# An edge-attention pass whose running sums stay in two PSUM banks, with small operations moved from VectorE to TensorE, ScalarE and GpSimd

## What is computed

```python
q = (xn @ Wq + bq).reshape(n, H, DH); k = ...; v = ...      # H = 8 heads of DH = 32
ep = ef @ We + be
scores = einsum('ehd,ehd->eh', q[dst], k[src] + ep[:, None, :]) * scale * ew[:, None]
m = segment_max(scores, dst)
ex = exp(scores - m[dst])
s = segment_sum(ex, dst)
out = segment_sum((ex / s[dst])[:, :, None] * v[src], dst)
```

## Time and profile before

| What | us |
|---|---|
| median of three runs | 3732.68 |
| lowest and highest | 3732.53, 3735.69 |
| the profiled execution's own time | 3734.78 |
| its span in the profile | 3733.0 |
| PE, DVE, ACT and POOL busy, whole span | 3127.7, 2161.4, 1687.2, 1888.5 |

### The profile page before, as it was taken

How to read it: one execution, slowest core, us unless ns; L and a number is a source line. 1 busy time by engine, 2 the same in 40 slices (tenths; PEclk the granted TensorE clock), 3 DMA queues, 4 the chain that set the end, 5 groups by cost and what they waited for, 6 DMA issues and landing times. The chain is left out here.

```text
span 3733.0 us, 52272 instructions
## 1 busy us (share of the span) xinstructions
PE 3127.7 (84%) x13504; PEld 2408.8 (65%) x13504; DVE 2161.4 (58%) x4835; ACT 1687.2 (45%) x3903; POOL 1888.5 (51%) x1845
## 2 busy tenths in 40 slices
PE   2778888788878689769859999999999999659798
PEld 2567666566665578646437777777777777436565
DVE  6333334333334600075569999999999999653515
ACT  1444333333334122233246676667676676332323
POOL 2777777777772044401046666666666666120010
PEclk8778767777778599979769999999999999779899
DMA  5555555555550167641067777777777777300000
GB/s 143 148 147 146 139 153 140 154 144 142 147 141 20 44 192 218 182 167 63 9 190 218 222 219 218 214 224 218 218 216 221 221 219 209 111 24 1 22 5 35
DMA packets 345535, 547.29 MB, mean 147 GB/s; under 512 B 170928, under 2 KB 222389, under 8 KB 344967
## 3 DMA queue, kind: packets, MB, share of 16 engines
q0 software_dynamic: 113216, 348.74, 32.8%
q1 hardware_dynamic: 224312, 183.42, 16.8%
q10 hardware_dynamic: 7743, 12.07, 1.0%
HBM read 493.32 MB, written 51.90 MB: 146 GB/s over the span
## 5 line engine op out<-in xcount | busy, mean ns | idle before, releaser
L2816 POOL DMA_INDIRECT store<-kv_d,src_of x832 | 872.4, 1049 | 414.6 <-issue 242.1
L821 POOL DMA_INDIRECT agg_rows<-xn_d,src_of x832 | 800.0, 962 | 268.7 <-issue 242.3
L993 PE MATMUL agg_sums<-agg_rows,agg_member 128*128 128x257 f32 x1664 | 578.0, 501 | 181.7 <-DVE acc L885 92.4
L834 ACT ACTIVATE agg_rows<-agg_rows,weight_of 128x256 f32<-128x256 f32 x832 | 373.0, 500 | 632.1 <-DMA agg_rows<-xn_d,src_of 631.5
L993 PEld LDWEIGHTS agg_sums<-agg_rows,agg_member 128*128 128x128 f32 x1664 | 387.7, 249 | 323.9 <-DVE acc L885 130.0
L885 DVE TENSOR_TENSOR acc<-acc,agg_sums 128x257 f32 x416 | 176.3, 424 | 598.9 <-PE agg_sums L993 598.0
L2840 PE MATMUL flash_query<-q,flash_mem_t 128*128 x1664 | 411.7, 391 | 48.3 <-DVE store L3045 37.7
L2853 PE MATMUL flash_sums<-store,flash_member 128*128 128x264 f32 x1664 | 422.8, 387 | 2.2 <-DVE store L3110 2.2
L2840 PEld LDWEIGHTS flash_query<-q,flash_mem_t 128*128 128x128 f32 x1664 | 312.7, 193 | 100.9 <-issue 54.6
L2853 PEld LDWEIGHTS flash_sums<-store,flash_member 128*128 128x128 f32 x1664 | 317.1, 191 | 56.1 <-issue 2.2
L3045 DVE TENSOR_TENSOR store<-store,flash_query 128x1024 f32<-128x1024 f32 x208 | 252.3, 1213 | 39.3 <-PE flash_query L2840 39.0
(11 more groups left out here) (468 smaller groups left out, 4574.3 us busy)
## 6 DMA issues: line engine op xcount, KB each, us to landing
moe_w<-in_L_ffn_W_dram SPq DMA_DIRECT2D x64, 512.0 KB
agg_feats<-in_ef_t_dram SPq DMA_DIRECT2D x104, 256.0 KB, 4.4
flash_goal<-goal_d SPq DMA_DIRECT2D x52, 512.0 KB, 4.4
agg_rows<-xn_d,src_of POOLq DMA_INDIRECT x832, 2.8
ep_d<-agg_ep SPq DMA_DIRECT2D x52, 256.0 KB
store<-kv_d,src_of POOLq DMA_INDIRECT x832, 4.1
flash_ep<-ep_d SPq DMA_DIRECT2D x416, 32.0 KB
flash_flags<-flags_d SPq DMA_DIRECT2D x416, 32.0 KB
```

The costliest lines, as they stand in the source:

```text
L821: pool.indirect_dma_start(rows[:, q, 0:D], None, sh.xn_d, bass.IndirectOffsetOnAxis(ap=sh.src_of[:, c:c + 1], axis=0)).then_inc(gathered[u ...
L834: act.activation(rows[:, q, 0:D], rows[:, q, 0:D], ACT.Copy, scale=sh.weight_of[:, bass.ds((UI * i + u) * SUBS + k, 1)]).then_inc(weighted, 1)
L993: last = pe.matmul(sums[:, j % 4, 0:W], member[:, c % (2 * BI * SUBS), :], rows[:, c % NB, :], start=(c % SUBS == 0), stop=(c % SUBS == SU ...
L2816: pool.indirect_dma_start(ring[:, s, :], None, sh.kv_d, bass.IndirectOffsetOnAxis(ap=sh.src_of[:, c:c + 1], axis=0)).then_inc(gathered[p][ ...
```

## The change

- The running sums of the current tile now stay in a PSUM bank, bank 1 or 2, chosen by a table made on the chip (`bank_id`): the bank changes each time the tile changes. `fold` is gone. An item's matmuls all accumulate. Ahead of each item PE issues a one-column matmul of zeros with the start flag (`clear_l`, `clear_r`) into column 511 of a bank: the item's own bank when it opens a new tile, bank 0, which holds nothing, otherwise (`open_id`). The flag lets the next matmuls overwrite the bank.
- `collect` now takes a group of two items. It waits until the items of the group before have been kept. `keep` waits for both items of its group, and an odd item's keep for the even one's; it still copies the bank to `sh.acc` after every item.
- `rescale` multiplies in the PSUM bank instead of in SBUF.
- From DVE to PE: the bar that picks a row's own sub-chunk is added by an identity matmul ahead of the carried values; scores minus maximum come from two matmuls, with `ident` and with `minus` (minus the identity), in place of a DVE subtraction and a PE transpose; `sh.work` is added to `down` by an identity matmul.
- From DVE to ACT: `diag`, the copy of `run`, and, once per window, the copy of `down` to `sh.work`. From DVE to POOL: `first_hot`, now with two buffers, behind a wait for the flags. The two products `z` become one.
- SP's `load` waits for `hot_ready` as well. DVE makes the tables before the first window, with some 17 small operations.

```diff
@@ stage_flash, PE
-                def collect(a, n):
-                    g = n // 2
+                def collect(a, g, banks, opened):
                     pe.wait_ge(member_ready, G * a.at + (g + 1))
                     pe.wait_ge(pv_ready, G * a.at + (g + 1))
-                    if n < 2:
-                        pe.wait_ge(added, WI * a.at + (n + 1))
-                    for k in range(SUBS):
-                        c = n % 2 * SUBS + k
-                        pe.matmul(sums[:, n % 3, 0:W], member[:, g % 2, c, :], ring[:, a.side * WS + 4 * g + c, HI_],
-                                  start=(k == 0), stop=False)
-
-                def fold(a, n, tiles):
...
+                    if g == 0:
+                        pe.wait_ge(rescaled, a.at + 1)
+                    if WI * a.at + 2 * g > 0:
+                        pe.wait_ge(added, WI * a.at + 2 * g)
+                    for n in (2 * g, 2 * g + 1):
+                        pe.matmul(sums[:, bass.ds(opened[n], 1), 511:512]..., clear_l[:, :], clear_r[:, :],
+                                  start=True, stop=True)
+                        for k in range(SUBS):
+                            c = n % 2 * SUBS + k
+                            last = pe.matmul(running(banks[n]), member[:, g % 2, c, :], ring[:, ..., HI_],
+                                             start=False, stop=(k == SUBS - 1), skip_group_check=True)
+                        last.then_inc(sums_done, 1)
...
                         pe.wait_ge(chain_ready, a.at + 1)
+                        pe.matmul(carried, sh.ident[:, :], bar..., start=True, stop=False)
                         pe.matmul(carried, head_row[:, :], carry...,
-                                  start=True, stop=True).then_inc(carry_ready, 1)
+                                  start=False, stop=True).then_inc(carry_ready, 1)
...
+                        pe.matmul(down[:, 0:D], sh.ident[:, :], sh.work[:, i, :], start=True, stop=False)
...
-                        pe.transpose(pt[:, 0:P], low[:, :], sh.ident[:, :])
+                        pe.matmul(pt[:, 0:P], sh.ident[:, :], scaled[:, :], start=True, stop=False)
+                        pe.matmul(pt[:, 0:P], top, minus[:, :], start=False, stop=True)
@@ stage_flash, ACT
-                def keep(a, n, tiles):
-                    act.wait_ge(sums_done, WI * a.at + (2 * WI + n + 1))
+                def keep(a, n, tiles, banks):
+                    act.wait_ge(sums_done, WI * a.at + (2 * WI + n // 2 * 2 + 2))
+                    if n % 2 == 1:
+                        act.wait_ge(added, WI * a.at + n)
                     act.activation(sh.acc[:, bass.ds(tiles[n], 1), :, :]...,
-                                   sums[:, n % 3, 0:W], ACT.Copy).then_inc(added, 1)
+                                   running(banks[n]), ACT.Copy).then_inc(added, 1)
```

More of the change, by code:

```diff
@@ L2679, in stage_flash @@
         scaled = sb("scaled", [P, WS * H])
-        ahead = sb("ahead", [P, P])
-        top = sb("top", [P, P])
-        low = sb("low", [P, P])
+        ahead_top = sb("ahead_top", [P, 2, P])
+        ahead, top = ahead_top[:, 0, :], ahead_top[:, 1, :]
+        outer = ahead_top[:, :, :].rearrange("p a n -> p (a n)")[:, P - 1:P + 1]
+        minus = sb("minus", [P, P])
         z = sb("z", [P, 2, WS])
@@ L2741, in stage_flash, with numbers, bank_numbers, open_numbers @@
         down_added = sem("down_added")
-        def tile_numbers(eng, w):
[L2745 to L2748, removed]
+        hot_ready = sem("hot_ready")
+        diag_ready = sem("diag_ready")
+        banks_ready = sem("banks_ready")
+        def numbers(eng, w, table, least, most):
+            _, values = nc.values_load_multi_w_load_instructions(
+                table[0:1, bass.ds(WI * w.at, WI)], engines=[eng.engine], min_val=least, max_val=most,
+                skip_runtime_bounds_check_because="the table was made on the chip within these bounds")
+            return values
+        def tile_numbers(eng, w):
+            return numbers(eng, w, sh.tile_id, 0, NT - 1)
+        def bank_numbers(eng, w):
+            return numbers(eng, w, bank_id, 1, 2)
+        def open_numbers(eng, w):
+            return numbers(eng, w, open_id, 0, 2)
+        def running(bank):
+            return sums[:, bass.ds(bank, 1), 0:W].rearrange("p a w -> p (a w)")
         def after(s):
@@ L2982, in body @@
                         belong(a, 0)
-                        tiles = tile_numbers(act, a)
+                        tiles, banks = tile_numbers(act, a), bank_numbers(act, a)
+                        act.wait_ge(chain_ready, a.at + 1)
+                        act.activation(diag[:, :], sh.ident[0:H, 0:H], ACT.Copy, scale=fall[:, 0:1]).then_inc(diag_ready, 1)
+                        act.activation(run[:, 0:1], run[:, WS:WS + 1], ACT.Copy)
                         act.wait_ge(back_ready, a.at + 1)
@@ L2990, in body @@
                     if a is not None:
-                        keep(a, 1, tiles)
+                        keep(a, 1, tiles, banks)
                         belong(a, 2)
-                        keep(a, 2, tiles)
+                        keep(a, 2, tiles, banks)
                     if s is not None:
                         place(s, 3)
+                    if ffn is not None:
+                        act.wait_ge(down_ready, 2 * i + (half + 2))
+                        act.activation(sh.work[:, i, :], down[:, 0:D], ACT.Copy).then_inc(down_added, 1)
                     if a is not None:
-                        keep(a, 3, tiles)
+                        keep(a, 3, tiles, banks)
                         belong(a, 3)
-                        keep(a, 4, tiles)
                     if more:
```

151 lines of the change are left out of this document (88 added, 63 removed).

## The result

| | before | after |
| --- | --- | --- |
| median of runs, us | 3732.61 (3731.63 to 3735.69) | 4036.89 (4036.58 to 4042.89) |
| ratio | | 1.0817, 95% interval 1.0803 to 1.083 |
| profiled span, us | 3733.0 | 4035.3 |
| period of the edge stage, us | 24.79 | 30.72 |

The account below looks back on a forecast made before the run. PE and DVE were both nearly full, neither the bound alone. PE's work of 20.5 us plus new waits of 6.3 gave a 26.8 us period, +102 us, and the clock +31: 3733.0 to 3866 us, range 3775 to 3955.

Parts of the forecast that it names:

- The round trips: PE stands still for ACT's keep and place ahead of the third and fourth asks, 2.18 us each per window.
- The price of a clear: Eight one-column zero matmuls per window on PE, 0.08 us each (ends 0 and 0.18), 0.64 per window.
- The clock: PE's stalls drop its clock in every third window or so: 0.6 us per window, 31 us in all.
- Rival 2: PE's clock falls at most stalls: 3940 to 4010 us, taken as 3960; chance 0.12.
- the wait for both copies of a pair: PE waits ahead of the fourth group's collects for both keeps of the third: 1.24 us.
- the wait ahead of the first collects: PE waits through exponentials, rescale and weigh, partly covered by the diagonal's matmuls and the ask: 0.7 us left.
- work rows: Adding sh.work into down on PE costs one 256-column matmul, 0.43 us per window.
- subtraction: Scores minus maximum as two PE matmuls instead of a transpose: +0.2 us per window, ends 0 and 0.3.
- bar: The bar added by a matmul on PE: 0.33 us per window, lower end 0.15.
- DVE's gain at nothing, its cover PE: DVE's 1.5 us less work per window counts as 0, since PE takes 26.8 us where DVE needs 21.5.
- the term that counts: DVE's gain of 1.5 us per window, said to count if PE's waits were absent.
- ACT, POOL and the start of the stage at nothing: ACT's added work, POOL's first_hot and DVE's 17 operations before the first window: each costed at 0.

Follow-up runs that it names:

- e1: The changed kernel with ACT's place for the third and fourth asks moved ahead of its copies (keep 0, keep 2): 3802.72 us, ratio 1.0179.
- e5: The changed kernel with each clear using the weights of the collect behind it, times a column of zeros: 4037.49 us, ratio 1.0805.
- e2_fill: The changed kernel with three useless matmuls into bank 0 ahead of the third and of the fourth ask: 3962.53 us, ratio 1.0602.
- e4: The kernel before, with its folds and copies kept and only the small operations moved off DVE: 3733.75 us, ratio 0.9999.
- g3: The changed kernel with banks and clears kept and all moved operations back on DVE: 4038.14 us, ratio 1.0815.
- g4: g1 with its remaining moved operations given back to DVE: 3828.79 us, ratio 1.0256.
- g1: The changed kernel with place first, shared clear weights, another order, work rows on DVE, half of down between back-to-back collects: 3740.81 us, ratio 1.0019.

## Why the prediction was wrong

The prediction's period was 26.8 us and 0.6 for the clock, 27.4; measured were 30.7.

- **The round trips** were right: predicted 2 x 2.18, measured 2.05 of idle time and a tail of 0.16 ahead of it, 2.21 each. e1 shows that they and what follows from them are most of the loss.
- **The price of a clear** failed. The prediction took 0.08 us with an upper end of 0.18, from an fp32 one-column matmul. Measured: 0.30, +1.8 us a window, 90 us in the sum. That these 90 us would come off the changed kernel without clears is not shown: no run took them out there. PE's weight loads (start, us) say why the price is what it is:

```profile
2502.26 0.09 PEld L2884 LDWEIGHTS flash_sums<-flash_clear_r,flash_clear_l 1*128 1x128 bf16 x1 [0.33 <-issue]
2502.36 0.74 PEld L2888 LDWEIGHTS flash_sums<-store,flash_member 128*128 128x128 f32 x4
```

  Before, the load of a collect started 0.2 us ahead of its first matmul (2419.15 against 2419.36 in the earlier trace rows), beside the matmul in front:

```profile
2419.15 0.85 PEld L2853 LDWEIGHTS flash_sums<-store,flash_member 128*128 128x128 f32 x4
```

  The clear lasts 0.10 us, so the next load has only 0.10 instead of 0.21 to lie beside, and 0.11 stand open. The clear's own load of 0.09 starts with the clear and not beside the collect ahead, and that is the other 0.09. Why it starts so late is open. The load of e5's fp32 clear starts 0.22 us ahead of its matmul at 2509.68:

```profile
2509.46 0.41 PEld L2883 LDWEIGHTS flash_sums<-flash_zero,flash_member 128*128 128x128 f32 x2
```

  Weights, their type and the number of passes differ at once between the two clears, and no run changes one alone. e5's clear costs 1.11 - 0.89 = 0.22: 0.14 of its own and 0.08 in the collect behind. The one of the earlier trace rows was no cheaper; the prediction misread it. It set the clear against the matmul ahead of it, but the cost is also in the matmul behind, which takes 0.68 us there where the one ahead takes 0.60. From clear to clear, with the row that follows those, it is 1720.28 - 1719.63 = 0.65, and 0.65 - 0.43 = 0.22:

```profile
1720.28 0.28 PE L2170 MATMUL mid_zsum<-ones,mid_kr 128*128 128x1 f32 x2
```

  The bf16 load itself took 91 ns on average; the Trainium skill (TensorE: Matmul & The Clock Gate, LDWEIGHTS) would give an estimated 107, so its figure was near, and the higher sum it gave was nearer the truth than the row I took.
- **The clock** failed too. Predicted a fall in every third window, 0.6 us; measured one in every window, 1.8 us, +61 us. I took the one place where the clock had fallen as the harder case, for having small matmuls around it. It fell here behind the second of two round trips 6.4 us apart. e2_fill shows that this is a price of its own, paid on top of the wait. Rival 2 was the nearest at 3960, but it too had the cheap clear.
- **The other terms**: the wait for both copies of a pair was 1.41 and a tail against 1.24, since ACT's second copy waits 0.2 us for the first; the wait ahead of the first collects 0.35 and a tail against 0.7, and it ended with ACT's `belong` (line 2981), not with DVE's `weigh` as predicted; work rows 0.54 against 0.43; subtraction 0.28 against 0.2; bar 0.24 against 0.33. Together +0.2 us.
- **DVE's gain at nothing, its cover PE** was wrong as a price of the moves. The prediction charged their work on PE in full, 0.33 + 0.43 + 0.2 = 0.96 us a window or 49 us, and set nothing against it. e4 and g3 put both together at nothing (about 1 us): DVE's gain was worth about what PE's new work cost. It did not show in the number, because the price of the banks was too low by more. Where the round trips are gone, DVE's gain is indeed "the term that counts": in g4 the moves undone cost 88 us, though PE has less to do.
- **ACT, POOL and the start of the stage at nothing**: no run takes these apart. The period explains 303 of the 304 us and its terms leave nothing for POOL; the first `scale` stands at 1929.3 us against 1937.7 before, so the start cost nothing.

So the steps that failed are the clear, priced at 0.08 us and measured at 0.30, and the clock, put at 0.6 us a window and measured at 1.8: 151 of the 171 us by which the forecast was low. An additive sum had a limit of its own. It would have made g1 without clears 90 us faster than g1 (measured 35) and e5 33 us faster than the changed kernel (0). In this loop of four engines a saving on one was first taken up by the wait next to it.

## What to carry to other kernels

When an accumulation in PSUM is made longer to spare a step, ask what waited for the step removed: here the fold let the copy out start after one item, and was cover for it besides. Price a tiny matmul by the distance from one to the next, the matmul behind it included, since the weight load behind it loses its cover. And where the clock depends on PE's stalls, move what is asked for ahead of what is merely stored, or fill the stall, before trimming PE's work: trimmed work went into longer stalls and a lower clock.

## What was not expected of the hardware

- More work made the kernel faster: 2.6 us a window of useless matmuls, 74 us less, with the clock at 0.98 for 0.94.
- Less work made it no faster: with ACT placing first and the clears left out, 2.4 us less of PE's work a window, the same 3803 us, with the clock at 0.96 for 1.00.
- Two of the chips ran the kernel before 18% slower than the others (4406 and 4404 against 3734 us). Their transfers were slower too; that these are the cause was not tested.
